# Four held down steps in token-tile order, and the second batch's residual additions on VectorE

## The chip, the core and the metric

The kernel runs on one core of a Trainium2 chip. The metric is the time of one execution on the device in microseconds (us), lower is better. PE is TensorE, DVE is VectorE, ACT is ScalarE, POOL is GpSimd, and SP is SyncE, which here only issues DMAs. The profile is that of one execution; L562 means line 562 of the kernel before.

## The reference

One block of a network, for two batches of 512 tokens with 512 features, all in float32. A conditioning vector gives shift, scale and gate for two layers:

```
mod = (silu(c) @ wmod).reshape(2, 6, 1, 512)
sa, ca, ga, sb, cb, gb = mod[:, 0] ... mod[:, 5]
ga, gb = sign * max(|.|, 0.25)
h = layernorm(x) * (1 + ca) + sa
x = x + ga * (h @ (weight * block_mask).T)
h = layernorm(x) * (1 + cb) + sb
gate = (h @ Wg.T) * ag
up   = (h @ Wu.T) * au
x = x + gb * ((silu(gate) * up) @ Wd.T) * ad
```

The inner width of the second layer is 1376, so it falls into 11 chunks of 128, the last of them short.

## The kernel before, in words

The first third masks the weights, computes the modulation and runs the first layer. The change lies in the second layer, the FFN. Its work is a list of 22 steps (`STEPS`): step s is batch s // 11 and chunk s % 11. A step has two halves on PE:

- gate/up (`gate_up`, matmuls at L726): 8 matmuls for the gate and 8 for the up product, each 128x512, into three PSUM banks taken in turn. Every product has two parts, high and low, since the activations are split into a rounded value and its remainder.
- down (`down`, matmuls at L780): for each of four token tiles t a product of 2 matmuls (high and low part), which accumulates over the 11 chunks of a batch in bank 4 + t. The whole step is 8 matmuls.

Between the halves of a step ScalarE takes the silu of the gate (L400) and rounds weights (`round_gu`, L361; `round_d`, L367). VectorE multiplies it with up (`inner`, L543), rounds the result (L550) and takes the remainder (L552). Rounded down weights stand in `whi_dn`, the split inner values in `in_split`; both have three slots, s % 3, and a slot is written again only when the down step that read it is over (`wait_down`). The activations of both batches, `ht`, stay in SBUF; those of batch 0 are last read by gate/up 10.

PE runs its program in the order of the loop at L898: gate/up of step s, then down of step s - 2 (`LAG`). For the last steps this changes: gate/up 21 follows down 18 directly, and down steps 19, 20 and 21 are held for `down_last` (L803), 12 products written out by hand. The first five need only steps 19 and 20; in front of the sixth PE waits for the inner values of step 21. Each step stands in the program twice, behind a branch, once with raw weights for weights that are exact and once with rounded ones. In these runs the branch steps over the first form.

Each bank, when its last product is done, is read by VectorE (`gate_ffn`, L562), which multiplies it by the gate and writes `xn`. Then `xn` is added to `xt`. For tiles n below `BY_POOL` = 6, that is all four of batch 0 and the first two of batch 1, GpSimd adds (L296) and SP issues the store (L245); for the last two VectorE adds (L626) and ScalarE issues the store (L416). There are no other GpSimd instructions in the FFN's second batch. Within VectorE's program the products of tiles 4, 5 and 6 come one after the other, then tile 6's addition, then product and addition of tile 7.

Of the kernel before, what the change touches and what calls it, by code (L numbers as in the profile page):

```python
# [29 lines left out]
P = 128  # L30
# [3 lines left out]
TT = 4  # L34
SEQ = TT * P
F = 1376
C = -(-F // P)
# [4 lines left out]
GATE_MIN = 0.25  # L42
STEPS = NB * C
WARM_UP = 18
BY_POOL = 6
H1_CHUNK = C + -NB * KT * SEQ // (3 * D)
LAG = 2

CHECKS_AT = {0: 3, 2: 1, 3: 2}

# [4 lines left out]
def gu_bank(s, u):  # L55


    return 3 if (s, u) == (1, 1) else (2 * s + u + 2) % 3


def adaln_block(nc, x, att_w, att_mask, cond, mod_ln1, mod_ln2, mod_gate, w_gu, w_gu_tail, w_down,
                scales, scales_tail, down_scale, out):
    with ExitStack() as ctx:
        def sb(name, shape, dt=F32):
            return ctx.enter_context(nc.sbuf_tensor(name, shape, dt))

        def sem(name):
            return ctx.enter_context(nc.semaphore(name))
# [4 lines left out]
        ht = sb("ht", [P, NB, KT, 2, SEQ], F32R)  # L73
# [3 lines left out]
        in_split = sb("in_split", [P, 3, 2, D], F32R)  # L77
# [4 lines left out]
        whi_dn = sb("whi_dn", [P, 3, D], F32R)  # L82
# [34 lines left out]
        def raw_d(c):  # L117
            return wffn[:, c, 2 * D:3 * D]

        def whi_d(s):  # L120
            return whi_dn[:, s % 3, :]


        bank = [ctx.enter_context(nc.psum_tensor(f"bank{i}", [P, D], F32)) for i in range(8)]
# [55 lines left out]
        wd_hi = sem("wd_hi")  # L180
        gate_mm = sem("gate_mm")
        up_mm = sem("up_mm")
# [3 lines left out]
        in_lo = sem("in_lo")  # L186
# [6 lines left out]
        def wait_down(eng, s):  # L193

            if s % C == C - 1:
                eng.wait_ge(acc_mm, TT * (s // C + 1))
            else:
                eng.wait_ge(down_mm, s - s // C + 1)
# [5 lines left out]
        def _(sp):  # L204
# [20 lines left out]
            for c in range(C):  # L225
# [14 lines left out]
                if c == 4:  # L240
                    sp.wait_ge(rows_done, KT + 1)
                    sp.dma_start(modw[:, 2, :, :], mod_gate[1]).then_inc(d_gate[1], 16)
            for n in range(BY_POOL):
                sp.wait_ge(out_ok, n + 1)
# [5 lines left out]
        def _(pool):  # L250
# [34 lines left out]
            for b in range(NB):  # L285
# [4 lines left out]
                if b == 0:  # L290

                    pool.wait_ge(att_done, NB * TT)
                    pool.memset(wffn[:, C - 1, :], 0.0).then_inc(tail_zero, 1)
            for n in range(BY_POOL):
                pool.wait_ge(acc_read, n + 1)
# [5 lines left out]
        def _(act):  # L301
# [27 lines left out]
            def modulate(n):  # L329

                q, k = divmod(n, KT)
                layer, b = divmod(q, NB)
                act.wait_ge(xt_done, n + 1)
                act.wait_ge(modc_ok, k + 1 if layer == 0 else KT + 1 + k // 2)
                if q < 2:
                    dst = h1[:, b, k, :]
                else:
                    dst = hbuf[:, n % 2, :]
                    if n >= 10:
                        act.wait_ge(h_lo, n - 9)  # L340
                src = bank[4 + n % 2] if q < 2 else bank[n % 2] if q == 2 else bank[3]
                act.activation(dst, src[:, :], ACT.Identity,  # L342
                               bias=modc[:, layer, k, 2 + b:3 + b],
                               scale=modc[:, layer, k, b:b + 1]).then_inc(h_ok, 1)
# [17 lines left out]
                   .then_inc(wgu_hi, 1)  # L362

            def round_d(s):
                if s >= 3:
                    wait_down(act, s - 3)
                act.activation(whi_d(s), raw_d(s % C), ACT.Copy).then_inc(wd_hi, 1)  # L367

# [20 lines left out]
            for s in range(STEPS):  # L389
# [22 lines left out]
                if 6 <= s < 10:  # L412
                    modulate(6 + s)
            for n in range(BY_POOL, NB * TT):
                act.wait_ge(out_last, n - BY_POOL + 1)
                act.dma_start(out[n * P:(n + 1) * P, :], xt[:, n, :]).then_inc(d_out, 16)  # L416
# [3 lines left out]
        def _(dve):  # L420
# [5 lines left out]
            for g in range(P // BLK):  # L426
                s = slice(g * BLK, (g + 1) * BLK)
# [55 lines left out]
            def split(n):  # L483

                b, k = divmod(n - NB * KT, KT)
                i = n - NB * KT + 1
                dve.wait_ge(h_ok, n + 1)
                dve.tensor_copy(ht[:, b, k, 0, :], hbuf[:, n % 2, :]).then_inc(h_hi, 1)
                dve.wait_ge(h_hi, i)
                dve.tensor_tensor(ht[:, b, k, 1, :], hbuf[:, n % 2, :],  # L490
                                  ht[:, b, k, 0, :].bitcast(F32), ALU.subtract).then_inc(h_lo, 1)
# [43 lines left out]
            def ffn_inner(s):  # L535
                c = s % C
                if s == 0:
                    dve.wait_ge(d_small, 48)
                dve.wait_ge(up_mm, s + 1)
                dve.wait_ge(silu_ok, s + 1)  # L540
                if s >= 2:
                    dve.wait_ge(in_lo, s - 1)
                dve.scalar_tensor_tensor(inner[:, s % 2, :], bank[gu_bank(s, 1)][:, :],  # L543
                                         scal[:, c, 1:2], silu_g[:, s % 2, :],
                                         ALU.mult, ALU.mult).then_inc(inner_ok, 1)
                dve.wait_ge(inner_ok, s + 1)
                if s >= 3:
                    wait_down(dve, s - 3)
                hi, lo = in_split[:, s % 3, 0, :], in_split[:, s % 3, 1, :]
                dve.tensor_copy(hi, inner[:, s % 2, :]).then_inc(in_hi, 1)  # L550
                dve.wait_ge(in_hi, s + 1)
                dve.tensor_tensor(lo, inner[:, s % 2, :], hi.bitcast(F32), ALU.subtract)\  # L552
                   .then_inc(in_lo, 1)

            def gate_ffn(b, t):
                n = b * TT + t
                dve.wait_ge(acc_mm, n + 1)
                dve.wait_ge(gate_ok, NB + b + 1)
                dve.wait_ge(xt_done, 4 * TT)
                if b:  # L560
                    dve.wait_ge(out_ok, TT)
                dve.scalar_tensor_tensor(xn[:, t, :], bank[4 + t][:, :], 2.0, gates[:, 2 + b, :],  # L562
                                         ALU.mult, ALU.mult).then_inc(acc_read, 1)
# [34 lines left out]
            for s in range(STEPS):  # L598
# [17 lines left out]
                if 6 <= s < 10:  # L616
                    split(6 + s)
                if s == C + LAG - 1:
                    for t in range(TT):
                        gate_ffn(0, t)  # L620
            for t in range(TT):
                n = TT + t
                gate_ffn(1, t)
                if n >= BY_POOL:
                    dve.wait_ge(acc_read, n + 1)
# [5 lines left out]
        def _(pe):  # L631
# [141 lines left out]
            def down_product(s, t, native):  # L773
                b, c = divmod(s, C)
                for part in range(2):
                    h = in_split[:, s % 3, part, t * P:(t + 1) * P]
                    w = whi_d(s)
                    if native:
                        h, w = h.bitcast(F32), raw_d(c)
                    last = pe.matmul(bank[4 + t][:, :], h, w, start=(c == 0 and part == 0),  # L780
                                     stop=(c == C - 1 and part == 1))
                if c == C - 1:
                    last.then_inc(acc_mm, 1)
                elif t == TT - 1:
                    last.then_inc(down_mm, 1)
# [16 lines left out]

            def down_last():  # L803

                o, a, z = STEPS - 3, STEPS - 2, STEPS - 1
                pe.wait_ge(in_lo, a + 1)
                pe.wait_ge(wd_hi, a + 1)

                def products(native):
                    for i, (s, t) in enumerate([(o, 0), (a, 0), (o, 1), (a, 1), (o, 2), (z, 0),  # L810
                                                (z, 1), (a, 2), (z, 2), (o, 3), (a, 3), (z, 3)]):
                        if i == 5:
                            pe.wait_ge(in_lo, z + 1)
                            pe.wait_ge(wd_hi, z + 1)
                        down_product(s, t, native)

                with pe.If(general[-1]):
                    products(True)
                with pe.Else():
                    products(False)  # L820
# [77 lines left out]
            for s in range(STEPS):  # L898
                if s == GROUPS[1][0]:
                    load_flag(1)  # L900
                if s == 0:
                    gate_up_first()
                else:
                    gate_up(s)
                if s == 4:
                    pe.wait_ge(cols_ok, 8)
                    flag_sum(1)
                if LAG <= s < STEPS - 1:
                    down(s - LAG)
                if s == 2:  # L910
                    pe.wait_ge(d_gate[1], 16)
                    pe.wait_ge(inner_ok, 2)
                    mod_rows(7, D, lambda j: modw[:, 2, j, :], bank[3])
                if s == 3:
                    pe.wait_ge(rows_copied, 8)
                    columns(2, KT, bank[3])
                if 6 <= s < 10:
                    transposes(6 + s)
                if s == 10:
                    pe.wait_ge(h_ok, 4 * TT)  # L920
                    gate_all(1, 0, bank[3])
                if s == 11:
                    pe.wait_ge(gate_ok, 3)
                    gate_all(1, 1, bank[3])
            down_last()


# [48 lines left out]
```

## Time and profile before

| | us |
|---|---|
| median of 3 runs | 185.62 |
| lowest, highest | 185.08, 185.81 |
| span of the profiled execution | 185.1 |
| PE busy | 176.7 (95%) |
| DVE busy | 91.8 (50%) |
| ACT busy | 84.8 (46%) |
| POOL busy | 32.3 (17%) |
| DMA, mean over the span | 115 GB/s |

The profiled execution has no other time than its span, from the first to the last instruction. "Busy" is the time in which an engine had an instruction under way. PE takes weights (row PEld) and multiplies at the same time, so the two rows overlap, and matmuls overlap one another: a single one lasts about 0.39 us from start to modelled end, but a new one starts every 0.23 us.

### The profile page before, as it was taken

The numbers are of one execution on the slowest core, as the hardware profiler recorded it, in microseconds if no ns is written. First come the engines' busy times: TensorE is split into PE (matmuls) and PEld (weight loads), VectorE is DVE, ScalarE is ACT, GpSimd is POOL, SyncE is SP. The second block draws the span as 40 slices with busy tenths as digits, with TensorE's granted clock in tenths as the row PEclk, the third lists the DMA queues.
The fourth block names the chain that finished last, engine by engine and source line by source line (L and its number), as shares of the span: only waits on it lengthen the run. The fifth ranks groups of instructions, "written<-read, shape, count | busy, mean of one in ns | idle before, by whom it ended". The sixth has DMA issues, their size and how long they took to land.

```text
span 185.1 us, 2333 instructions
## 1 busy us (share of the span) xinstructions
PE 176.7 (95%) x808; PEld 130.2 (70%) x808; DVE 91.8 (50%) x191; ACT 84.8 (46%) x118; POOL 32.3 (17%) x42
## 2 busy tenths in 40 slices
PE   6879999999999999999999999999999999999990
PEld 6645454634558768878888888888888888888860
DVE  3843364286195896444444646128742224444274
ACT  3031312757979958824266434553444333342200
POOL 1440331093009330000000000002800000000040
PEclk9987999999999999999999999999999999999997
DMA  6999999996008600000000000000410000000005
GB/s 178 377 403 398 420 410 400 413 402 237 0 2 262 209 4 0 0 4 4 0 4 0 0 5 0 4 4 0 170 60 0 4 4 0 2 4 0 4 9 218
DMA packets 9203, 21.34 MB, mean 115 GB/s; under 512 B 2432, under 2 KB 2432, under 8 KB 8672
## 3 DMA queue, kind: packets, MB, share of 16 engines
q1 hardware_dynamic: 8352, 20.52, 29.3%
q10 hardware_dynamic: 832, 0.54, 0.9%
q8 instruction: 15, 0.25, 0.5%
q14 instruction: 4, 0.03, 0.1%
HBM read 18.96 MB, written 2.10 MB: 114 GB/s over the span
## 4 chain that ended last, share of the span: by engine, by line
PE 90%; DVE 3%; DMA 2%; issue 1%; SPq 1%; DVEq 0%
PE bank L726 43%; PE bank L780 21%; PE bank L696 16%; PE bank L680 3%; PE bank L637 3%; DMA xt<-in_x 2%; PE bank L650 2%; PE bank L704 1%; DVE xn L451 1%; DVE xn L562 1%; SPq L206 1%; DVE msum L456 1%; DVE xt L626 0%; DVE bns L438 0%; PE bank L664 0%
## 5 line engine op out<-in xcount | busy, mean ns | idle before, releaser
L726 PE MATMUL bank<-ht,whi_gu 128*128 128x512 f32 x352 | 84.6, 393 | 0.0
L726 PEld LDWEIGHTS bank<-ht,whi_gu 128*128 128x128 f32 x352 | 65.4, 188 | 14.9 <-issue 1.7
L543 DVE SCALAR_TENSOR_TENSOR awork<-bank,scal,awork 128x512 f32<-128x512 f32 x22 | 16.5, 751 | 54.4 <-PE bank L726 51.5
L780 PE MATMUL bank<-whi_dn,in_split 128*128 128x512 f32 x176 | 43.4, 390 | 0.0
L780 PEld LDWEIGHTS bank<-whi_dn,in_split 128*128 128x128 f32 x176 | 32.9, 188 | 7.0 <-DVE in_split L552 0.2
L696 PE MATMUL bank<-awork,wffn 128*128 128x512 f32 x64 | 32.6, 623 | 0.0
L400 ACT ACTIVATE awork<-bank,scal 128x512 f32<-128x512 f32 x22 | 15.1, 688 | 32.2 <-PE bank L726 31.7
L361 ACT ACTIVATE whi_gu<-wffn 128x1024 fp32r<-128x1024 f32 x22 | 23.2, 1055 | 6.6 <-PE bank L726 6.6
L296 POOL TENSOR_TENSOR xt<-xt,xn 128x512 f32<-128x512 f32 x6 | 7.8, 1319 | 104.0 <-DVE xn L562 104.0
L696 PEld LDWEIGHTS bank<-awork,wffn 128*128 128x128 f32 x64 | 11.0, 198 | 9.9 <-issue 9.2
L552 DVE TENSOR_TENSOR in_split<-awork,in_split 128x512 fp32r<-128x512 f32 x22 | 16.2, 737 | 0.8
L354 ACT ACTIVATE junk<-wffn 128x1536 uint8<-128x1536 uint16 x11 | 16.3, 1480 | 0.5
L367 ACT ACTIVATE whi_dn<-wffn 128x512 fp32r<-128x512 f32 x22 | 13.7, 622 | 0.0
L438 DVE BATCH_NORM_STATS2 bns<-xt 128x6 f32<-128x512 f32 x16 | 10.9, 681 | 2.8 <-DMA xt<-in_x 2.1
L320 ACT ACTIVATE rows<-bank 128x256 f32<-128x256 f32 (+1 forms) x8 | 3.9, 490 | 18.0 <-PE bank L637 18.0
L342 ACT ACTIVATE hbuf<-bank,modc 128x512 f32<-128x512 f32 x8 | 6.1, 774 | 12.5 <-PE bank L680 12.5
L277 POOL TENSOR_TENSOR xt<-xt,xn 128x512 f32<-128x512 f32 x8 | 10.0, 1281 | 8.1 <-DVE xn L521 8.1
L342 ACT ACTIVATE wffn<-bank,modc 128x512 f32<-128x512 f32 x8 | 6.2, 776 | 10.5 <-DVE modc L480 8.2
L680 PEld LDWEIGHTS bank<-ident,xn 128*128 128x128 f32 x64 | 7.8, 142 | 4.2 <-issue 3.5
L550 DVE CAST in_split<-awork 128x512 fp32r<-128x512 f32 x22 | 9.5, 430 | 0.8
L680 PE MATMUL bank<-ident,xn 128*128 128x128 f32 x64 | 9.3, 273 | 0.0
L451 DVE TENSOR_SCALAR xn<-xt,mv,rstd 128x512 f32<-128x512 f32 x16 | 7.8, 543 | 0.6 <-POOL rstd L264 0.6
(50 smaller groups left out, 89.8 us busy)
## 6 DMA issues: line engine op xcount, KB each, us to landing
wffn<-in_w_gu SPq DMA_DIRECT2D x10, 512.0 KB, 9.9
wffn<-in_w_down SPq DMA_DIRECT2D x10, 256.0 KB, 11.1
xt<-in_x SPq DMA_DIRECT2D x8, 256.0 KB, 6.7
modw<-in_mod_ln SPq DMA_DIRECT2D x4, 512.0 KB, 7.0
modw<-in_mod_gate SPq DMA_DIRECT2D x2, 1024.0 KB, 11.5
modw<-in_mod_ln SPq DMA_DIRECT2D x2, 1024.0 KB, 9.9
out<-xt SPq DMA_DIRECT2D x6, 256.0 KB, 2.0
maskt<-in_att_mask SPq DMA_DIRECT2D x4, 256.0 KB, 6.3
```

Source lines behind the costliest of these rows:

```text
L342: act.activation(dst, src[:, :], ACT.Identity, bias=modc[:, layer, k, 2 + b:3 + b], scale=modc[:, layer, k, b:b + 1]).then_inc(h_ok, 1)
L354: act.activation(junk[:, :], low, ACT.Copy, accum_out=chk[:, c:c + 1])\
L361: act.activation(whi_gu[:, s % 2, :], wffn[:, s % C, 0:2 * D], ACT.Copy)\
L367: act.activation(whi_d(s), raw_d(s % C), ACT.Copy).then_inc(wd_hi, 1)
L400: act.activation(silu_g[:, s % 2, :], bank[gu_bank(s, 0)][:, :], ACT.Silu, scale=scal[:, s % C, 0:1]).then_inc(silu_ok, 1)
L438: dve.bn_stats(bns[:, q, t, :], xt[:, n % (NB * TT), :]).then_inc(bn_done, 1)
L543: dve.scalar_tensor_tensor(inner[:, s % 2, :], bank[gu_bank(s, 1)][:, :], scal[:, c, 1:2], silu_g[:, s % 2, :], ALU.mult, ALU.mult).then_i ...
L552: dve.tensor_tensor(lo, inner[:, s % 2, :], hi.bitcast(F32), ALU.subtract)\
L680: last = pe.transpose(dst[:, t * P:(t + 1) * P], xn[:, t, k * P:(k + 1) * P], ident[:, :])
L696: last = pe.matmul(bank[4 * b + t][:, :], h1[:, b, k, t * P:(t + 1) * P], awork[:, k, :], start=(k == 0), stop=(k == KT - 1))
L726: return pe.matmul(bank[gu_bank(s, u)][:, :], w, h, start=(k == 0 and part == 0), stop=(k == KT - 1 and part == 1))
L780: last = pe.matmul(bank[4 + t][:, :], h, w, start=(c == 0 and part == 0), stop=(c == C - 1 and part == 1))
```

## The change

`HELD = 4`: down step 18 is held too, so that gate/up 21 follows gate/up 20 directly, and `down_last` has 16 products. In the new order the first five are (18,0), (19,0), (20,0), (18,1), (19,1); then comes the wait for step 21; then (21,0), (20,1), (21,1); then all four products of tile 2 and all four of tile 3. Since the slots of step 18 are then still in use, step 21 puts its rounded weights and inner values into the part of `ht` that held batch 0. `BY_POOL` becomes 4 (`TT`): VectorE makes all four residual additions of batch 1, and ScalarE issues their four stores.

```diff
-BY_POOL = 6
+BY_POOL = TT
+HELD = 4
         def whi_d(s):
-            return whi_dn[:, s % 3, :]
+            return ht[:, 0, 1, 0, :] if s == STEPS - 1 else whi_dn[:, s % 3, :]
+
+        def inner_part(s, part):
+            return ht[:, 0, 0, part, :] if s == STEPS - 1 else in_split[:, s % 3, part, :]
...
             def round_d(s):
-                if s >= 3:
+                if s == STEPS - 1:
+                    act.wait_ge(up_mm, C)
+                elif s >= 3:
                     wait_down(act, s - 3)
...
-                if s >= 3:
+                if 3 <= s < STEPS - 1:
                     wait_down(dve, s - 3)
-                hi, lo = in_split[:, s % 3, 0, :], in_split[:, s % 3, 1, :]
+                hi, lo = inner_part(s, 0), inner_part(s, 1)
...
             def down_last():
 
-                o, a, z = STEPS - 3, STEPS - 2, STEPS - 1
+                o, p, a, z = range(STEPS - HELD, STEPS)
                 pe.wait_ge(in_lo, a + 1)
                 pe.wait_ge(wd_hi, a + 1)
 
                 def products(native):
-                    for i, (s, t) in enumerate([(o, 0), (a, 0), (o, 1), (a, 1), (o, 2), (z, 0),
-                                                (z, 1), (a, 2), (z, 2), (o, 3), (a, 3), (z, 3)]):
-                        if i == 5:
-                            pe.wait_ge(in_lo, z + 1)
-                            pe.wait_ge(wd_hi, z + 1)
-                        down_product(s, t, native)
+                    for s in (o, p, a):
+                        down_product(s, 0, native)
+                    for s in (o, p):
+                        down_product(s, 1, native)
+                    pe.wait_ge(in_lo, z + 1)
+                    pe.wait_ge(wd_hi, z + 1)
+                    down_product(z, 0, native)
+                    for s in (a, z):
+                        down_product(s, 1, native)
+                    for t in (2, 3):
+                        for s in (o, p, a, z):
+                            down_product(s, t, native)
...
-                if LAG <= s < STEPS - 1:
+                if LAG <= s < STEPS - HELD + LAG:
                     down(s - LAG)
```

The program of PE before, from down 18 to the end. L770 ends gate/up 21; L817 is the branch of `down_last`; `wffn` holds the raw weights, `whi_dn` the rounded ones.

```order
L780 MATMUL bank7<-whi_dn,in_split 128x512 x2
L799 UNCONDITIONAL_BRANCH
...
L770 UNCONDITIONAL_BRANCH
L817 COMPARE_AND_BRANCH
...
L817 UNCONDITIONAL_BRANCH
L780 MATMUL bank4<-whi_dn,in_split 128x512 x4
L780 MATMUL bank5<-whi_dn,in_split 128x512 x4
L780 MATMUL bank6<-whi_dn,in_split 128x512 x2
L780 MATMUL bank4<-whi_dn,in_split 128x512 x2
L780 MATMUL bank5<-whi_dn,in_split 128x512 x2
L780 MATMUL bank6<-whi_dn,in_split 128x512 x4
L780 MATMUL bank7<-whi_dn,in_split 128x512 x6
```

The same place now, from the end of gate/up 20. L774 is the branch of gate/up 21, L829 that of `down_last`, and L732 and L786 are the matmuls of before's L726 and L780.

```order
L732 MATMUL bank1<-ht,whi_gu 128x512 x8
L776 UNCONDITIONAL_BRANCH
L774 COMPARE_AND_BRANCH
...
L829 UNCONDITIONAL_BRANCH
L786 MATMUL bank4<-whi_dn,in_split 128x512 x6
L786 MATMUL bank5<-whi_dn,in_split 128x512 x4
L786 MATMUL bank4<-ht 128x512 x2
L786 MATMUL bank5<-whi_dn,in_split 128x512 x2
L786 MATMUL bank5<-ht 128x512 x2
L786 MATMUL bank6<-whi_dn,in_split 128x512 x6
L786 MATMUL bank6<-ht 128x512 x2
L786 MATMUL bank7<-whi_dn,in_split 128x512 x6
L786 MATMUL bank7<-ht 128x512 x2
```

Eight matmuls went from in front of gate/up 21 into the closing block. Ten matmuls still stand in front of the first that reads step 21's values; behind them 22 follow where 14 did, and each of banks 6 and 7 gets its eight in one piece.

The end of VectorE's program before; `bank4` to `bank7` are the four token tiles of batch 1.

```order
L562 SCALAR_TENSOR_TENSOR xn<-bank4,maskt 128x512
L562 SCALAR_TENSOR_TENSOR xn<-bank5,maskt 128x512
L562 SCALAR_TENSOR_TENSOR xn<-bank6,maskt 128x512
L626 TENSOR_TENSOR xt<-xt,xn 128x512
L562 SCALAR_TENSOR_TENSOR xn<-bank7,maskt 128x512
L626 TENSOR_TENSOR xt<-xt,xn 128x512
```

And now, where L568 is before's L562 and L632 its L626:

```order
L568 SCALAR_TENSOR_TENSOR xn<-bank4,maskt 128x512
L632 TENSOR_TENSOR xt<-xt,xn 128x512
L568 SCALAR_TENSOR_TENSOR xn<-bank5,maskt 128x512
L632 TENSOR_TENSOR xt<-xt,xn 128x512
L568 SCALAR_TENSOR_TENSOR xn<-bank6,maskt 128x512
L632 TENSOR_TENSOR xt<-xt,xn 128x512
L568 SCALAR_TENSOR_TENSOR xn<-bank7,maskt 128x512
L632 TENSOR_TENSOR xt<-xt,xn 128x512
```

Two additions came in, each directly behind its product and ahead of the product of the next bank; on GpSimd the six instructions of L296 become four.

## Rows read from the trace of the kernel before

**Rows 1.** Page: busy us (share of the span) and instructions of each engine.

```profile
PE 176.7 (95%) x808; PEld 130.2 (70%) x808; DVE 91.8 (50%) x191; ACT 84.8 (46%) x118; POOL 32.3 (17%) x42
```

**Rows 2.** Page: share of the chain that ended last, by engine.

```profile
PE 90%; DVE 3%; DMA 2%; issue 1%; SPq 1%; DVEq 0%
```

**Rows 3.** The chain in order of time: start us, us, what.

```profile
110.22 3.68 PE bank L726 x16
...
169.24 1.81 PE bank L780 x8
171.05 3.63 PE bank L726 x16
174.68 4.16 PE bank L780 x18
178.84 0.02 issue
178.86 0.70 DVE xn L562
...
179.72 1.52 issue
181.24 0.69 DVE xn L562
...
181.96 0.69 DVE xt L626
```

**Rows 4.** Windows, PE alone: stretch, us, busy (instructions), granted clock, DMA share, GB/s.

```profile
174.70:180.20 5.50, 5.50 (x24) 1.00 0.00 0
```

**Rows 5.** Timeline of the end: start us, us, engine, line, operation, [idle before].

```profile
174.51 5.68 PE L780 MATMUL bank<-whi_dn,in_split 128*128 128x512 f32 x24
174.72 0.75 DVE L543 SCALAR_TENSOR_TENSOR awork<-bank,scal,awork 128x512 f32<-128x512 f32 x1 [3.50 <-PE bank L726]
...
175.96 0.69 DVE L552 TENSOR_TENSOR in_split<-awork,in_split 128x512 fp32r<-128x512 f32 x1
176.71 3.06 PEld L780 LDWEIGHTS bank<-whi_dn,in_split 128*128 128x128 f32 x14 [0.19 <-DVE in_split L552]
177.47 2.08 DVE L562 SCALAR_TENSOR_TENSOR xn<-bank,maskt 128x512 f32<-128x512 f32 x3 [0.82 <-PE bank L780]
178.24 2.53 POOL L296 TENSOR_TENSOR xt<-xt,xn 128x512 f32<-128x512 f32 x2 [44.63 <-DVE xn L562]
...
179.59 1.73 DVE L626 TENSOR_TENSOR xt<-xt,xn 128x512 f32<-128x512 f32 x1
```

**Rows 6.** Stores: issue ns min/median/max, landing us.

```profile
L416 ACTq DMA_DIRECT2D out<-xt x2: 350/358/367, 181.4 to 182.7; - x2
...
DMA to landing us min/median/max: 2.1/2.1/2.2
```

**Rows 7.** Timeline in the middle of the kernel, where batch 0 ends.

```profile
128.38 5.23 POOL L296 TENSOR_TENSOR xt<-xt,xn 128x512 f32<-128x512 f32 x4 [59.33 <-DVE xn L562]
132.50 1.66 DVE L552 TENSOR_TENSOR in_split<-awork,in_split 128x512 fp32r<-128x512 f32 x1
```

**Rows 8.** All instances of three lines: duration in ns, min/median/max, first and last start.

```profile
L552 DVE TENSOR_TENSOR in_split<-awork,in_split x22: 691/693/1664, 62.1 to 176.0; 128x512 fp32r<-128x512 f32 x22
L562 DVE SCALAR_TENSOR_TENSOR xn<-bank,maskt x8: 678/681/692, 127.6 to 181.2; 128x512 f32<-128x512 f32 x8
L296 POOL TENSOR_TENSOR xt<-xt,xn x6: 1280/1291/1471, 128.4 to 179.5; 128x512 f32<-128x512 f32 x6
```

**Rows 9.** Timeline of steps 19 and 20 on ScalarE and VectorE.

```profile
163.84 0.75 DVE L543 SCALAR_TENSOR_TENSOR awork<-bank,scal,awork 128x512 f32<-128x512 f32 x1 [3.50 <-PE bank L726]
163.89 1.06 ACT L361 ACTIVATE whi_gu<-wffn 128x1024 fp32r<-128x1024 f32 x1 [0.67 <-PE bank L726]
167.46 0.69 ACT L400 ACTIVATE awork<-bank,scal 128x512 f32<-128x512 f32 x1 [2.50 <-PE bank L726]
170.52 0.69 DVE L552 TENSOR_TENSOR in_split<-awork,in_split 128x512 fp32r<-128x512 f32 x1
```

More of the change, by code:

```diff
@@ L775, in down_product @@
                 for part in range(2):
-                    h = in_split[:, s % 3, part, t * P:(t + 1) * P]
+                    h = inner_part(s, part)[:, t * P:(t + 1) * P]
                     w = whi_d(s)
```

## The prediction

> **What bounds the kernel now.** I read the page's busy row first: PE is at work 176.7 of 185.1 us, 95% [rows 1], and the chain that ended last runs over PE for 90% of the span [rows 2]. The change touches neither the loads nor the number of matmuls, so the question is only what the last two steps and the tail do.
>
> The chain in order of time gives the beat of the main loop [rows 3]: 3.63 us for 16 gate/up matmuls and 1.81 us for 8 down matmuls, or 0.2265 us per matmul, with no gap between the steps, although each begins with a branch. The granted clock there is 1.00, TensorE's 2.4 GHz level [rows 4]. Behind the 18th of the 24 closing matmuls the chain leaves PE at 178.84 and stays on VectorE to the end: `xn` (L562) 0.70 us, `xt` (L626), a stretch of 1.52 us that the chain calls "issue", then `xn` 0.69 and `xt` 0.69, ending at 182.65. The span ends at 185.1, so 2.45 us lie behind it: the last store, which lands 2.1 us after its issue [rows 6], and the closing waits.
>
> The timeline shows what the 1.52 us are [rows 5]. PE starts its 24 closing matmuls at 174.51 and is done 5.68 us later, at 180.19. Product and addition of the last tile could follow at once. But VectorE is inside the addition of token tile 2, an operation with two SBUF inputs, which lasts 179.59 to 181.32: 1.73 us, where the same addition for tile 3 takes 0.69. What differs is GpSimd: its two additions run 178.24 to 180.77, the second from about 179.49 (1.28 us each). The same happens in the middle of the kernel [rows 7]: GpSimd adds four tiles from 128.38 to 133.61, and VectorE's `in_split` subtraction, again two SBUF inputs, takes 1.66 us at 132.50 where the usual one takes 0.69 (median 693 ns, longest 1664 [rows 8]). The product of L562, one PSUM input and one SBUF input, keeps its 0.68 to 0.69 us beside GpSimd in all 8 instances. So the last addition but one stands still until 181.32 - 0.69 = 180.63, when GpSimd is nearly through, and it holds up the product of the last bank: it starts at 181.24 and not at 180.22.
>
> **The change part by part.**
> 1. Down step 18 moves behind gate/up 21. PE executes the same matmuls (24 + 8 before, 32 now [rows 3, 5]), so 8 x 0.2265 = 1.81 us move and none are added. By the chain gate/up 21 starts at 169.24 rather than 171.05, if its inputs allow. They do: its rounded weights are ready at 163.89 + 1.06 = 164.95; its second half needs the silu of step 20, which runs at 167.46 to 168.15, while that half starts 1.81 us into the step, at 171.05; the `inner` value of step 19 is there at 163.84 + 0.75 = 164.59 [rows 9]. VectorE's last step-20 subtraction ends at 170.52 + 0.69 = 171.21, and gate/up 21 then ends at 174.68 - 1.81 = 172.87. No wait appears.
> 2. The cover for the last `inner` remains five products, 10 matmuls or 2.26 us. The work it hides (product, rounding and remainder on VectorE, 174.72 to 175.96 + 0.69 = 176.65 [rows 5]) moves 1.81 earlier with gate/up 21. PE's wait in front of the sixth product is 0.19 us of weight loading before, of which the matmul starts show 0.09 (24 starts would take 23 x 0.2265 + 0.39 = 5.60 and took 5.68). I take the same after: 0 change. Bounds: at best the 0.09 goes, at worst the whole 0.19 shows, +0.10.
> 3. The roundings of step 21 write to `ht` of batch 0. ScalarE's last rounding follows the last silu at once, and both now come 1.81 earlier; its new wait, for gate/up 10, was met at 110.22 + 3.68 = 113.9 [rows 3]. VectorE drops a wait that was long met. 0.
> 4. The branch pair of down(18) goes, and the branch ahead of the closing block steps over 32 matmuls instead of 24. The removed pair showed no gap: 0. The longer step over is not in the trace; steps over 8, 16 and 24 show none, so 0, with a bound in the rivals.
> 5. The order. PE ends at 180.19 as before, since the same matmuls stand before that end. After the wait come z0; a1, z1; then four products for tile 2 and four for tile 3. Bank 4's product started at 177.47 before, so 175.66 now. Bank 5 is ready 4 matmuls later, 176.57; bank 6 another 8 later, 178.38; bank 7 at 180.20.
> 6. VectorE now does four additions, GpSimd none, so each should take the 0.69 us of the free instance. From one product to its addition takes 0.73 us (178.86 to 179.59), and the next product can start 0.08 before an addition ends (181.24 against 181.32), so a pair costs 0.73 + 0.61 = 1.34. Products then start at 175.66; 177.00 (VectorE busy until then, bank ready 176.57); 178.38; and 180.22. The third pair is over at 179.72: 0.50 us of slack before the last bank. The last addition is 180.22 + 0.72 = 180.94 to 181.63. Cover gone: each additional microsecond of VectorE work beyond that slack would count in full. Bounds for one of the three earlier additions: 0.69 and 1.73.
> 7. All four stores of the second batch come from ScalarE's queue, at an issue of 0.35 to 0.37 us each [rows 6]. They are due 1.3 us or more apart, at about 177.0, 178.4, 179.8 and 181.7, so none waits; ScalarE has no other instruction behind its last rounding. The last two were issued at 181.4 and 182.7 before and landed in 2.1 and 2.2 us; now they are 1.8 apart. 0, bounds -0.1 (2.2 becomes 2.1) and +0.37 (one issue in the way).
>
> Sum: the last addition ends at 181.63 instead of 182.65: -1.02 us. The span becomes 184.1. The median of the three runs is 185.62, the profiled span 185.1 and the lowest run 185.08, so the profile is at the fast end of the same population; I carry the difference over: 185.62 - 1.02 = 184.60.
>
> **A rule weighed.** The Trainium skill, page "SBUF — State Buffer", section "SBUF: two separate sides", says that a VectorE operation with two SBUF inputs and a GpSimd operation that reads SBUF lock the same port pair for a whole instruction, and that whichever starts first gets it while the other fully blocks. By that rule the addition would have run from 180.77 to 181.46, and the row ends 0.14 earlier; otherwise the trace agrees. Since the sum takes the end of before from its row, it is the same by both. "Whichever starts first" is what rival A rests on, which can be told from rows alone.
>
> **Rivals.**
> A. The race (10%). Who stands still depends on who came first, and GpSimd's second addition began only 0.10 us before VectorE's. If in most unprofiled executions VectorE comes first, its addition is 179.59 to 180.28; GpSimd then holds until 181.56, the last product is at 180.26, and the last addition waits until about 181.42 (0.14 before GpSimd's end, as in the row) and ends at 182.11. Then the kernel before has only 0.48 us to lose: 185.14. For: the runs spread over 0.73 us, and one of GpSimd's six additions took 1471 ns where the shortest took 1280 [rows 8], so it too can be held. Against: both starts hang on the same PE beat, so the 0.10 should hold.
> B. The long addition isn't GpSimd's doing but that of the first such addition (5%), for instance because it is new code. Then add0 is 1.73, the pairs start at 175.66, 178.04, 179.38 and 180.72, and the last ends at 182.13: gain 0.52, time 185.1. Against: `in_split`, an old instruction, had the same stretch beside GpSimd.
> C. PE runs dry (5%, the slower side). The place is the branch before the closing block, now over 32 matmuls with their weight loads. If the code behind it has to be fetched then, PE stands for about one small transfer, which the stores show at 2.1 us; everything behind shifts by it: 185.62 - 1.02 + 2.1 = 186.7. It takes over 1.95 us of standstill to make the kernel slower by 0.5%. For: no row shows a step over so long a block. Against: the chain has no gap at the branches of the last steps, the one over 24 matmuls included.
> D. The end is set by something beside both (5%): an early sign would be a last store that lands later because three others are in its queue. 0.35 us of issue for each of two waiting stores, 0.7 us: 185.3. Against: the spacing of step 7.
>
> **How the numbers follow.** Forecast 75%, A 10%, B 5%, C 5%, D 5%. About 0.5% (0.93 us) is what a measurement can tell from no change. My 1.02 us is only 0.09 above that. With 0.1 to 0.2 us of error in the terms of steps 2, 6 and 7 and in the medians, the forecast lands above the line 7 times in 10: 0.53, plus 0.03 from A and B where the medians err my way: faster 0.56. Same: 0.22 + 0.17 = 0.39. Slower 0.05. The forecast's own range is 184.3 to 184.9. The runs of one kernel spread over 0.7 us and the comparison may find another level, so downwards I go to 184.05; upwards A, B and D reach 185.3, and I end at 185.4, which leaves out C and a little.
>
> **What would show it.** Right: no GpSimd additions after 135 us; gate/up 21 starting near 169.2 on the chain, no PE gap but the 0.1 to 0.2 at the sixth closing product; closing matmuls ending at 180.2; four L632 additions of 0.69 us; the last product (L568) within 0.05 us of the last matmul's end; the chain on PE until there, with no "issue" of over 0.1; span near 184.1. Wrong: an addition above 1 us without GpSimd (B), a hole in PE's row at about 172.9 (C), a PE wait over 0.3 at the sixth product (step 2), stores landing in over 2.3 us (D), or all of this right and the timed runs apart by only half of it (A).

## The result and the profile after

| | before | after |
|---|---|---|
| median of 20 runs, us | 185.66 | 184.51 |
| lowest | 185.08 | 184.15 |
| ratio of the times, after to before, 95% interval | | 0.9948 (0.9929 to 0.9967) |
| span of the profiled execution | 185.1 | 182.4 |
| last matmul's end to the last addition's end, in the trace | 2.46 | 1.44 |

The changed kernel is 0.5% faster, 1.15 us by the medians. The ratio puts it at 0.97 us, with 0.6 to 1.3 us in its interval. The two profiled spans are 2.7 us apart, and that is not what the change does. The executions of this kernel differ at their start (below), so the two traces have to be compared piece by piece and not by their spans.

The chain of the changed kernel, in order of time (start us, us, what), its last pieces:

```profile
158.42 3.63 PE bank L732 x16
162.04 1.81 PE bank L786 x8
163.86 7.25 PE bank L732 x32
171.11 7.35 PE bank L786 x32
178.46 0.02 issue
178.48 0.70 DVE xn L568
179.18 0.02 issue
179.21 0.69 DVE xt L632
```

Gate/up 20 and 21 are one piece of 32 matmuls, 7.25 us, and the closing block is another of 32. Against [rows 3] the "issue" of 1.52 us is gone: the last product starts 0.02 us behind PE. The same on the timeline (start us, us, engine, line, operation), from the closing block on:

```profile
170.95 2.43 PE L786 MATMUL bank<-whi_dn,in_split 128*128 128x512 f32 x10
...
173.14 0.30 PEld L786 LDWEIGHTS bank<-ht 128*128 128x128 f32 x2 [0.19 <-DVE ht L558]
...
173.91 0.69 DVE L568 SCALAR_TENSOR_TENSOR xn<-bank,maskt 128x512 f32<-128x512 f32 x1 [0.82 <-PE bank L786]
...
174.63 0.69 DVE L632 TENSOR_TENSOR xt<-xt,xn 128x512 f32<-128x512 f32 x1
175.24 0.69 DVE L568 SCALAR_TENSOR_TENSOR xn<-bank,maskt 128x512 f32<-128x512 f32 x1
...
175.96 0.69 DVE L632 TENSOR_TENSOR xt<-xt,xn 128x512 f32<-128x512 f32 x1
...
176.67 0.69 DVE L568 SCALAR_TENSOR_TENSOR xn<-bank,maskt 128x512 f32<-128x512 f32 x1
177.39 0.69 DVE L632 TENSOR_TENSOR xt<-xt,xn 128x512 f32<-128x512 f32 x1
...
178.48 0.69 DVE L568 SCALAR_TENSOR_TENSOR xn<-bank,maskt 128x512 f32<-128x512 f32 x1 [0.39 <-PE bank L786]
```

Ten matmuls run ahead of the wait, the wait for the last inner value has its 0.19 us as in [rows 5], and the four additions take 0.69 us each. The second pair starts 1.33 us behind the first because VectorE is busy until then, the third and fourth when their banks are ready. VectorE is idle 0.39 us ahead of the last one.

All four stores from one queue do no harm (issue and landing of L422; duration in ns, min/median/max):

```profile
L422 ACTq DMA_DIRECT2D out<-xt x4: 338/344/366, 175.4 to 179.9; - x4
...
DMA to landing us min/median/max: 2.0/2.1/2.1
```

**Where the 2.7 us of span lie.** From the start of gate/up 20 to the end of the last addition it is 165.61 to 182.65 before, 17.04 us, and 163.86 to 179.90 after, 16.04: 1.00 us from the change. Behind the last addition both have 2.48 us. The other 1.75 us are there before gate/up 20 starts, where both kernels execute the same program. A table of PE in a stretch of the start (stretch, us, busy and matmuls, granted clock, DMA share, GB/s), before:

```profile
12.50:16.00 3.50, 3.50 (x13) 0.51 1.04 396
```

and after:

```profile
12.50:16.00 3.50, 3.50 (x20) 1.00 1.04 396
```

In the profile before, TensorE was granted half its clock over nearly all of this stretch, the 1.2 GHz level, and began 13 matmuls in it; after, it had 2.4 GHz and began 20. The same group of eight modulation products starts at 12.37 us before and 12.21 after, ahead of the stretch; the next such group starts at 19.05 and 17.24, behind it: 0.16 us apart, then 1.81. The mean clock over the span is 0.986 in the profile before and 0.998 in the one after. In every run for which both are on record the time is 1.7 to 1.9 us above the span (184.18 against 182.4 in the profiled one after), so the profile before belongs to a run of about 186.9 us and not to a typical one. Runs with a mean clock below 0.993 are mostly over 1 us longer than the others of their kernel, so where they shift a median, that of the runs at 0.993 and above is given too.

### The profile page after: what moved, and what is told of

It reads as the page before. It is cut to its first block, busy times and chain, and to the rows that moved or that the text cites. A ratio compares the mean times of both kernels' runs of the same rounds, so it can differ in the third digit from the quotient of the medians.

```text
span 182.4 us, 2330 instructions
## 1 busy us (share of the span) xinstructions
PE 175.9 (96%) x808; PEld 130.4 (71%) x808; DVE 92.2 (51%) x193; ACT 84.9 (47%) x118; POOL 29.8 (16%) x40
## 4 chain that ended last, share of the span: by engine, by line
PE 92%; DVE 4%; DMA 2%; issue 0%; SPq 0%
PE bank L732 44%; PE bank L786 22%; PE bank L702 16%; PE bank L686 3%; PE bank L643 3%; DMA xt<-in_x 2%; PE bank L656 2%; PE bank L710 1%; DVE xn L457 1%; DVE bns L444 1%; DVE msum L462 1%; SPq L210 0%; DVE xn L568 0%; DVE xt L632 0%; PE bank L670 0%
## 5 line engine op out<-in xcount | busy, mean ns | idle before, releaser
L732 PE MATMUL bank<-ht,whi_gu 128*128 128x512 f32 x352 | 84.5, 393 | 0.0
L732 PEld LDWEIGHTS bank<-ht,whi_gu 128*128 128x128 f32 x352 | 65.4, 188 | 15.0 <-issue 1.6
L786 PE MATMUL bank<-whi_dn,in_split 128*128 128x512 f32 x168 | 41.8, 390 | 0.0
L786 PEld LDWEIGHTS bank<-whi_dn,in_split 128*128 128x128 f32 x168 | 31.5, 188 | 6.6
L702 PE MATMUL bank<-awork,wffn 128*128 128x512 f32 x64 | 31.5, 604 | 0.0
L558 DVE TENSOR_TENSOR in_split<-awork,in_split 128x512 fp32r<-128x512 f32 x21 | 15.5, 739 | 0.7
L300 POOL TENSOR_TENSOR xt<-xt,xn 128x512 f32<-128x512 f32 x4 | 5.2, 1338 | 59.4 <-DVE xn L568 59.4
L373 ACT ACTIVATE whi_dn<-wffn 128x512 fp32r<-128x512 f32 x21 | 13.1, 622 | 0.0
L346 ACT ACTIVATE hbuf<-bank,modc 128x512 f32<-128x512 f32 x8 | 6.1, 775 | 12.5 <-PE bank L686 12.5
L281 POOL TENSOR_TENSOR xt<-xt,xn 128x512 f32<-128x512 f32 x8 | 10.0, 1290 | 8.1 <-DVE xn L527 8.1
L556 DVE CAST in_split<-awork 128x512 fp32r<-128x512 f32 x21 | 9.0, 431 | 0.7
L853 PE MATMUL bank<-ident 128*128 128x128 f32 x36 | 7.1, 390 | 1.5 <-POOL ident L258 1.5
```

The costliest lines, as they stand in the source:

```text
L346: act.activation(dst, src[:, :], ACT.Identity, bias=modc[:, layer, k, 2 + b:3 + b], scale=modc[:, layer, k, b:b + 1]).then_inc(h_ok, 1)
L702: last = pe.matmul(bank[4 * b + t][:, :], h1[:, b, k, t * P:(t + 1) * P], awork[:, k, :], start=(k == 0), stop=(k == KT - 1))
L732: return pe.matmul(bank[gu_bank(s, u)][:, :], w, h, start=(k == 0 and part == 0), stop=(k == KT - 1 and part == 1))
```

## The experiments

All compare with the kernel before on the same chip. The lines of the tail are read in each profile, since the start varies by more than the effect.

**Only the additions.** One number of the kernel before:

```diff
-BY_POOL = 6
+BY_POOL = TT
```

> The kernel before with one number changed: all four additions of the second batch on VectorE, down steps and their order as before. Theory T (the end is set by VectorE's queue behind the last bank; GpSimd costs only while one of its additions lies over one of VectorE's): four pairs of product and addition at 1.34 us from bank 4 on put the last product at 181.49 and the end of the last addition at 182.90 in the times of the trace before, 2.71 us behind the last matmul's end where before had 2.46. So +0.25 us against before, no gain. Rival R (taking GpSimd out of the tail is what gains): the last addition ends 1.46 us behind the last matmul as in the changed kernel, -1.0 us.

Measured: ratio 1.0003 (0.9983 to 1.0022), no gain. The end of VectorE's timeline:

```profile
177.98 0.69 DVE L562 SCALAR_TENSOR_TENSOR xn<-bank,maskt 128x512 f32<-128x512 f32 x1 [0.82 <-PE bank L780]
178.71 0.69 DVE L626 TENSOR_TENSOR xt<-xt,xn 128x512 f32<-128x512 f32 x1
179.32 0.68 DVE L562 SCALAR_TENSOR_TENSOR xn<-bank,maskt 128x512 f32<-128x512 f32 x1
...
180.04 0.69 DVE L626 TENSOR_TENSOR xt<-xt,xn 128x512 f32<-128x512 f32 x1
180.64 0.68 DVE L562 SCALAR_TENSOR_TENSOR xn<-bank,maskt 128x512 f32<-128x512 f32 x1
181.36 0.69 DVE L626 TENSOR_TENSOR xt<-xt,xn 128x512 f32<-128x512 f32 x1
181.97 0.68 DVE L562 SCALAR_TENSOR_TENSOR xn<-bank,maskt 128x512 f32<-128x512 f32 x1
182.69 0.69 DVE L626 TENSOR_TENSOR xt<-xt,xn 128x512 f32<-128x512 f32 x1
```

No addition is slow any more, but the four pairs stand one behind the other at 1.34, 1.32 and 1.33 us, and the last ends at 183.38, 2.72 us behind PE (180.66). Banks 4, 5 and 6 are ready only 0.45 and 0.91 us apart in this order, less than a pair takes, so VectorE never catches up. One stall has been exchanged for a queue of about the same size (2.46 us before). R falls; T's 2.71 is met in the trace. Its +0.25 us of time is inside the interval and not shown by it.

**Only the order.** The changed kernel with `BY_POOL = 6` again.

> The changed kernel with tiles 4 and 5 of the second batch given back to GpSimd: four held steps in tile order alone. T: GpSimd's two additions are over at about 177.2 in the times of the trace after, before VectorE's addition of tile 6 starts at 177.4, so all of VectorE's additions take 0.69 and the last ends 1.46 us behind the last matmul: the whole gain, 1.0 us below before, equal to the changed kernel. R: GpSimd's additions are back, so a VectorE addition takes about 1.7 us and the gain goes: within 0.3 us of before.

Measured: ratio 0.9938 (0.9915 to 0.9961), median 184.27: the whole gain. In its timeline:

```profile
176.60 2.54 POOL L300 TENSOR_TENSOR xt<-xt,xn 128x512 f32<-128x512 f32 x2 [42.81 <-DVE xn L568]
...
178.56 0.69 DVE L568 SCALAR_TENSOR_TENSOR xn<-bank,maskt 128x512 f32<-128x512 f32 x1 [1.12 <-PE bank L786]
179.28 0.69 DVE L632 TENSOR_TENSOR xt<-xt,xn 128x512 f32<-128x512 f32 x1
...
180.37 0.69 DVE L568 SCALAR_TENSOR_TENSOR xn<-bank,maskt 128x512 f32<-128x512 f32 x1 [0.40 <-PE bank L786]
```

GpSimd is through at 179.14, VectorE's addition starts at 179.28, so the two no longer overlap, with 0.14 us to spare. What keeps them apart is that bank 6 is ready 8 matmuls (1.81 us) behind bank 5, where it was 4 (0.91 us) before. In this order the old split of the additions is as good as the new one. The last addition ends 1.44 us behind PE.

**GpSimd's two additions left out.**

```diff
-            for n in range(BY_POOL):
+            for n in range(TT):
                 pool.wait_ge(acc_read, n + 1)
...
-                sp.wait_ge(out_ok, n + 1)
+                sp.wait_ge(out_ok if n < TT else acc_read, n + 1)
```

> The kernel before without GpSimd's two additions of the second batch (tiles 4 and 5 are stored without the second layer's contribution; the stores wait for VectorE's products instead). T: VectorE's addition of tile 6 takes 0.69 instead of 1.73 us, the last addition ends 1.46 us behind the last matmul, -1.0 us against before. Rival B (the first such addition is slow by itself, GpSimd has no part in it): still 1.7 us, no change.

Measured: ratio 0.9927 (0.9904 to 0.9949). The rows that answer to [rows 5]:

```profile
176.08 2.06 DVE L562 SCALAR_TENSOR_TENSOR xn<-bank,maskt 128x512 f32<-128x512 f32 x3 [0.82 <-PE bank L780]
...
178.17 0.69 DVE L626 TENSOR_TENSOR xt<-xt,xn 128x512 f32<-128x512 f32 x1
178.80 0.69 DVE L562 SCALAR_TENSOR_TENSOR xn<-bank,maskt 128x512 f32<-128x512 f32 x1
```

The first addition is not slow by itself, B falls. With GpSimd quiet the old order ends 1.45 us behind PE too. Its banks 6 and 7 are 6 matmuls (1.36 us) apart, and that is enough for one pair.

**GpSimd busy, but not reading.**

```diff
+                if n >= TT:
+                    pool.memset(wffn[:, n - TT, :], 0.0).then_inc(out_ok, 1)
+                    continue
                 pool.tensor_tensor(xt[:, n, :], xt[:, n, :], xn[:, n % TT, :], ALU.add)\
```

> The kernel before with GpSimd's two additions of the second batch replaced by two memsets of 128x1536 on a free tensor, which took 1.39 us in the trace before and read nothing (tiles 4 and 5 are stored without the second layer's contribution). T with the rule of the Trainium skill, page SBUF — State Buffer, section on the two sides (a VectorE operation with two SBUF inputs meets only a GpSimd operation that reads SBUF): VectorE's addition takes 0.69, -1.0 us. Rival G (any GpSimd instruction stops it): the memsets end at about 181.0, the addition at 181.6, the last one ends 2.7 us behind the last matmul, +0.3 us.

Measured:

```profile
176.34 2.71 POOL L297 MEMSET wffn<- 128x1536 f32 x2 [44.61 <-DVE xn L565]
177.68 0.69 DVE L629 TENSOR_TENSOR xt<-xt,xn 128x512 f32<-128x512 f32 x1
```

The memsets run 176.34 to 179.05, right over VectorE's addition, and it keeps its 0.69 us; the last addition ends 1.45 us behind PE. G falls: a GpSimd instruction that only writes SBUF doesn't stop it. That agrees with the rule of the Trainium skill, page SBUF — State Buffer, section on the two sides, by which only a GpSimd operation that reads SBUF meets such an addition. But memset and addition differ in more than that, and no run has a GpSimd instruction with one SBUF input there. The time by itself doesn't show T's -1.0 us: the ratio is 0.9976 (0.9948 to 1.0005). Its seven runs at a clock of at least 0.993 have a median of 184.47, the like runs of before 185.59, which is -1.1 us. The trace decides here.

**The cost put back into the changed kernel.**

```diff
+            pool.wait_ge(acc_read, NB * TT - 1)
+            for i in range(2):
+                pool.tensor_tensor(maskt[:, i, :].bitcast(F32), hbuf[:, 0, :], hbuf[:, 1, :], ALU.add)
```

> The changed kernel with two GpSimd additions of scratch tensors (128x512, SBUF to SBUF, result unused) that start behind VectorE's product of tile 6 and depend on nothing else: the suspected cost put back. T: they take 1.28 us each, the second lies over VectorE's last addition, which starts at 179.2 in the times of the trace after and stands until shortly before GpSimd is done. If VectorE's addition of tile 6 comes first (it starts 0.03 us behind its product, GpSimd's 0.09), GpSimd runs 178.1 to 180.6 and the last addition ends near 181.2, +1.3 us against the changed kernel; if GpSimd comes first, near 180.6, +0.7. Rival (the gain came from the order of the products alone, contention has no part in it): no change.

Measured: median 186.42, ratio to before 1.0026 (0.9988 to 1.0064). Only four of its ten runs had a clock of at least 0.993; their median is 185.3, where the like runs of the changed kernel have 184.45, +0.85 us. In its timeline:

```profile
177.41 0.69 DVE L635 TENSOR_TENSOR xt<-xt,xn 128x512 f32<-128x512 f32 x1
177.46 3.00 POOL L304 TENSOR_TENSOR maskt<-hbuf 128x512 f32<-128x512 f32 x2 [45.61 <-DVE xn L571]
...
178.50 0.69 DVE L571 SCALAR_TENSOR_TENSOR xn<-bank,maskt 128x512 f32<-128x512 f32 x1 [0.40 <-PE bank L789]
179.23 1.78 DVE L635 TENSOR_TENSOR xt<-xt,xn 128x512 f32<-128x512 f32 x1
```

VectorE's addition came 0.05 us first and took its 0.69, and GpSimd's pair took 3.00 us where the same two additions took 2.53 in the kernel before and 2.54 with only the order changed. The longer one was GpSimd's first, 1.78 us; its second, from 179.2, took 1.25. That one started just ahead of VectorE's last addition (179.23), which took 1.78: both engines can be the one that stands. The end moves from 179.90 to 181.01, +1.11 us, between T's two cases (+0.7 and +1.3); the order was that of the first case, but GpSimd was held about 0.46 us and not 0.6. The rival falls: with the order of the products unchanged, most of the gain is gone.

**Bank 6 later.**

```diff
-                    for t in (2, 3):
-                        for s in (o, p, a, z):
-                            down_product(s, t, native)
+                    for s, t in ((o, 2), (p, 2), (a, 2), (o, 3), (p, 3), (z, 2), (a, 3), (z, 3)):
+                        down_product(s, t, native)
```

> The changed kernel with (21, 2) moved behind (18, 3) and (19, 3), so that bank 6 is ready 4 matmuls (0.91 us) and not 8 (1.81 us) ahead of bank 7; nothing else moves. T with the pair cost of 1.34 us: the last product starts 1.34 - 0.91 = 0.43 us behind the last matmul's end, the last addition ends 1.89 instead of 1.46 us behind it, +0.43 us against the changed kernel. Rival: VectorE's slack was larger than 0.5 us, then under 0.2.

Measured, VectorE's last three and PE's last group:

```profile
177.35 0.69 DVE L568 SCALAR_TENSOR_TENSOR xn<-bank,maskt 128x512 f32<-128x512 f32 x1 [0.92 <-PE bank L786]
177.61 0.62 PE L786 MATMUL bank<-ht 128*128 128x512 f32 x2
178.08 0.69 DVE L632 TENSOR_TENSOR xt<-xt,xn 128x512 f32<-128x512 f32 x1
178.69 0.68 DVE L568 SCALAR_TENSOR_TENSOR xn<-bank,maskt 128x512 f32<-128x512 f32 x1
179.41 0.69 DVE L632 TENSOR_TENSOR xt<-xt,xn 128x512 f32<-128x512 f32 x1
```

PE ends at 178.23 and the last addition at 180.10, 1.87 us later, where T had 1.89 and the changed kernel 1.44; the rival falls. At 0.91 us between the last two banks the last product waits for VectorE; at 1.36 (the old order with GpSimd quiet) and at 1.81 (grouped by tile) it doesn't. So the distance has to be about one pair, 1.34 us. In time it is 184.66 against 184.51, the ratio to before is 0.9948 (0.9912 to 0.9984), and T's +0.43 us can't be told from that.

**A candidate to beat both.** Six products ahead of the wait, and the last addition and store in two column halves:

```diff
-                    for s in (o, p):
+                    for s in (o, p, a):
                         down_product(s, 1, native)
...
+                    for h in range(2):
+                        w = slice(h * D // 2, (h + 1) * D // 2)
+                        dve.tensor_tensor(xt[:, n, w], xt[:, n, w], xn[:, t, w], ALU.add)\
+                           .then_inc(out_last, 1)
...
+            sp.wait_ge(out_last, NB * TT - BY_POOL)
+            sp.dma_start(out[n * P:(n + 1) * P, 0:D // 2], xt[:, n, 0:D // 2]).then_inc(d_out, 16)
```

> A candidate to beat both: the changed kernel with six products ahead of the wait instead of five ((20,1) drawn forward), and the last tile's addition and store cut into two column halves, the left half's store from SP and the right half's from ScalarE. T: the wait at the sixth product (0.09 us in matmul starts) goes; two half additions cost about 0.15 us more than one (estimate from a fixed part of some 0.15 in the 0.69); the last store carries half the bytes, 0.33 us less at the 0.66 us that 256 KB occupy the DMA engines. Sum -0.25 us against the changed kernel, just about what can be seen. Rival: a store's time is nearly all fixed (it lands after 2.0 to 2.1 us though the engines are busy 0.7), and then the two additions make it +0.05 us.

Measured: ratio 0.9902 (0.9866 to 0.9938), median 184.11, lowest 183.78; the changed kernel had 184.51 and 184.15. On the chain and among the DMA issues (KB each, us to landing):

```profile
163.93 7.25 PE bank L744 x32
171.19 7.27 PE bank L798 x32
```

```profile
out<-xt SPq DMA_DIRECT2D x1, 128.0 KB, 1.8
out<-xt ACTq DMA_DIRECT2D x1, 128.0 KB, 1.8
```

The closing block takes 7.27 instead of 7.35 us, so the wait at the sixth product has gone. The two half additions end at 179.96, 1.51 us behind PE instead of 1.44, so cutting the addition cost 0.07 us and not 0.15. The half stores land in 1.8 us instead of 2.0 to 2.1, and the span ends 2.22 us behind the last addition instead of 2.48. The rival, that a store's time is nearly all fixed, falls: half the bytes took about 0.3 us off. Added up, -0.08 + 0.07 - 0.26 = -0.27 us, where T had -0.25; by the medians -0.4. The two intervals overlap, so that it beats the changed kernel rests on the rows and on medians of separate measurements. It is the fastest complete kernel of the study.

**More warm-up.** The changed kernel with `WARM_UP = 21`.

> The changed kernel with 21 warm-up products instead of 18 on PE at the start. The profiles of before, and of the first two runs of this study, show TensorE at a granted clock of 0.50 from about 10.5 to 13.9 us, after PE had stood 0.8 us at 7.8 us; those of the changed kernel and the next two don't. Theory W (that gap decides): three more products fill it where the clock rises early, the runs with a granted clock under 0.99 become rarer and the median falls by 0 to 0.5 us. Rival: the gap has no part in it, or the added products delay the first real matmul (8.6 us) where the clock rises late: +0.3 us and the same share of slow starts.

The stretch named there is misread: by the windows above it lies between 12.5 and 16.0 us. Measured: median 184.61, ratio 0.9944 (0.9918 to 0.9970). The median didn't fall. In the trace the first real matmul starts at 8.86 us instead of 8.62 and gate/up 20 at 164.18 instead of 163.86, 0.32 us later: as the rival had it, the added products cost where the clock doesn't fall. The lowest clock of its 12 runs is 0.991, where the changed kernel had three of 20 below that (0.988 and twice 0.981, 186.3 to 187.5 us). Whether a fallen clock becomes rarer can't be said from 12 runs: the two variants before this one, with 18 warm-up products, had none below 0.994 in 19 runs. And W's gap doesn't decide alone. In the kernel without the two GpSimd additions PE stood longer ahead of its first real matmul (1.44 us) than in the profile before (0.83), and its clock didn't fall:

```profile
8.76 0.64 PE L637 MATMUL bank<-modw,sc 128*32 128x256 f32 x8 [1.44 <-DMA modw<-in_mod_ln]
```

What decides it stays open.

## Why the prediction was right

Forecast 184.60, measured 184.51. The sum of -1.02 us is met by the traces at -1.00 and by the ratio at -0.97; the medians are 1.15 apart. Set to the times of the trace before (1.75 us added), the four products of VectorE start at 175.66, 176.99, 178.42 and 180.23, where the prediction had 175.66, 177.00, 178.38 and 180.22, and the last addition ends at 181.65, where it had 181.63. By its own steps:

1. The move (steps 1, 3 and 4). Gate/up 21 followed at once, 32 matmuls in 7.25 us; no wait, and no gap at the branch over 32 matmuls. C didn't happen. The chain runs from 163.86 through 171.11 to 178.46 without a piece of waiting in between.
2. The cover (step 2). 0.19 us before and after. That it was a real cost is shown by the candidate: with a sixth product ahead of the wait the closing block takes 7.27 us, where the four traces with five products ahead of it have 7.31 to 7.37.
3. The cause of the 1.52 us. Right, and now shown from three sides: GpSimd's additions left out, the long addition goes; replaced by memsets that overlap it, it goes as well; put back into the changed kernel, it returns with 1.78 us.
4. VectorE's queue (steps 5 and 6). Pairs at 1.33 to 1.34 us as worked out. The slack is 0.47 us instead of 0.50: the last two products start 178.48 - 176.67 = 1.81 us apart, and a pair takes 1.34. The idle time of 0.39 in the timeline is the same slack, counted from the recorded end of the addition, 0.08 us later than a next product could start.
5. The stores (step 7). 2.0 to 2.1 us, 0. D didn't happen.
6. The race, A. It needs VectorE to come first in most executions of the kernel before. The gain would have been 0.48 us then; the interval of 0.6 to 1.3 us leaves that out. The kernel before has one trace, so how often GpSimd came first isn't counted. What A says of the lock itself, that whoever comes first makes the other wait, did show up in the changed kernel with GpSimd's cost put back.

What the prediction didn't say is which part of the change brings the gain. It worked out a stall that goes with GpSimd's additions, and that reads as if `BY_POOL` did it. Measured alone, that edit brings nothing and the order brings everything. Leaving GpSimd's additions out is enough too, but giving them to VectorE in the old order is not: its queue takes what the stall gave back. With the numbers of steps 5 and 6 this could have been worked out beforehand.

One step failed, without harm: how the profile stands to the median. I took the span of 185.1 as a time, beside the lowest run of 185.08, and called the profile the fast end of the runs. A time is about 1.8 us longer than its span, so that profile was one whose clock had fallen at the start, about 186.9. Only because the term was carried as a difference did the median's 185.62 keep the forecast right; the span forecast of 184.1 missed the 182.4 for that reason. The granted clock would have warned of it, but its window was laid over the end alone [rows 4].

A smaller misreading: of the eight products of L562 only five ran beside GpSimd. The first of each batch was over before GpSimd's first addition (178.16 against 178.24 in the second), and the last started 0.47 us behind GpSimd's end. That such a product isn't held rests on those five.

## What to carry to other kernels

Where the last accumulators of a kernel are drained by pairs of operations, space their completions by at least one pair (1.34 us here); the last should find its engine idle. If a VectorE addition with both inputs in SBUF is two times too long, look for a GpSimd addition over it that reads SBUF, and see whether shifting either in time is enough before moving work: moving it may only turn the stall into a queue. And compare two profiles from a common landmark to the end, with the granted clock of the start beside it, before reading anything from the difference of their spans.

## What the runs showed of the hardware

- The hold works both ways. Beside VectorE's addition GpSimd's were held as well: a pair took 3.00 us where it takes 2.53 to 2.54. VectorE's held addition ends 0.55 us behind GpSimd's recorded end, 0.14 less than its own 0.69, in all three cases: 134.16 for 133.61 and 181.32 for 180.77 in the kernel before, 181.01 for 180.46 in the one with the cost put back.
- A memset of 128x1536 on GpSimd over a VectorE addition cost that addition nothing (0.69 us).
- A store of 128 KB with 1 KB per row landed in 1.8 us, one of 256 KB with 2 KB per row in 2.0 to 2.2.
- TensorE was granted half the clock between 12.5 and 16 us in some executions (before, only the additions, only the order: 0.51 to 0.55) and not in others (after, GpSimd's two left out: 1.00), with the same program up to there; the profiles before and after stand 1.75 us apart ahead of the change, more than the change itself brings.
